# Flamingo block on one core: queries of the cross-attention halved in row layout and turned by DMA instead of on TensorE

## The reference

```python
x = x + tanh(g_xattn) * attention(layernorm(x), ctx, ctx, mask)   # softmax(q k^T / 8 + mask) v, 4 query heads share one k, v
x = x + tanh(g_ffn) * ffn(layernorm(x))                           # router, top 8 of 512 slots, gate
```

## Time and profile before

| | us |
|---|---|
| median of 3 runs (lowest, highest) | 1191.7 (1190.68, 1191.79) |
| the profiled execution | 1189.83 |
| its span | 1187.9 |
| busy in the span: PE, VectorE, ScalarE, GpSimd | 1141.3, 946.4, 918.8, 888.4 |
| first 40 us (loads, first layernorm, pipeline fills): PE busy | 24.39 |
| attention windows 1 to 63, from the first reciprocal L1217 at 39.44 to the last at 885.36 | 845.9 |

### The profile page before, as it was taken

How to read it: one execution, slowest core, us unless ns; L and a number is a source line. 1 busy time by engine, 2 the same in 40 slices (tenths; PEclk the granted TensorE clock), 3 DMA queues, 4 the chain that set the end, 5 groups by cost and what they waited for, 6 DMA issues and landing times.

```text
span 1187.9 us, 35060 instructions
## 1 busy us (share of the span) xinstructions
PE 1141.3 (96%) x14385; PEld 912.3 (77%) x14642; DVE 946.4 (80%) x2255; ACT 918.8 (77%) x1230; POOL 888.4 (75%) x797
## 2 busy tenths in 40 slices
PE   4999999999999999999999999999999999999997
PEld 3888888888888888888888888888877565555553
DVE  5988888887888888888888888888874888766765
ACT  5898998988988898898898889989862344555544
POOL 5999999999999999999999999999970001503222
PEclk9999999999999999999999999999999999999999
DMA  9421231142124213311421221131237100011223
GB/s 340 141 68 48 62 110 54 42 107 71 41 55 103 75 41 68 116 48 41 104 71 52 58 58 42 50 73 47 70 103 262 81 1 1 1 72 72 107 107 142
DMA packets 60735, 95.09 MB, mean 80 GB/s; under 512 B 35233, under 2 KB 44449, under 8 KB 56482
## 3 DMA queue, kind: packets, MB, share of 16 engines
q1 hardware_dynamic: 59858, 91.79, 25.1%
q10 hardware_dynamic: 720, 1.05, 0.3%
HBM read 71.75 MB, written 20.97 MB: 78 GB/s over the span
## 4 chain that ended last, share of the span: by engine, by line
PE 70%; POOL 16%; DVE 8%; issue 3%; ACT 2%; DMA 1%; DVEq 0%; SPq 0%; POOLq 0%
PE psum L913 13%; PE psum L890 12%; POOL arena L577 11%; PE psum L966 8%; PE psum L920 6%; PE psum L901 6%; PE psum L943 6%; PE psum L937 5%; PE psum L938 5%; PE psum L1044 2%; POOL arena L545 2%; PE psum L868 2%; PE psum L953 1%; PE psum L980 1%; POOL arena L594 1%
## 5 line engine op out<-in xcount | busy, mean ns | idle before, releaser
L577 POOL TENSOR_TENSOR arena<-arena 128x768 bf16<-128x768 f32 x448 | 652.6, 1472 | 43.4 <-ACT arena L699 41.5
L1283 DVE CUSTOM_DVE_ANT_0 arena<-psum,arena 128x750 f32<-128x750 f32 x448 | 420.5, 939 | 127.7 <-PE psum L901 122.0
L699 ACT ACTIVATE arena<-psum 128x768 f32<-128x768 f32 x448 | 362.6, 809 | 87.8 <-PE psum L920 87.7
L703 ACT ACTIVATE arena<-arena,neg_max 128x750 f32<-128x750 f32 x448 | 410.9, 917 | 4.2 <-DVE neg_max L1283 4.2
L913 PE MATMUL psum<-ident,arena 128*128 128x128 f32 x1792 | 268.4, 272 | 0.0
L937 PEld LDWEIGHTS psum<-arena 128*128 128x128 bf16 (+1 forms) x2688 | 194.7, 98 | 57.5
L890 PE MATMUL psum<-arena 128*128 128x512 bf16 x674 | 221.9, 383 | 14.2
L938 PE MATMUL psum<-arena 128*128 128x64 bf16 (+1 forms) x2688 | 222.0, 193 | 0.0
L937 PE MATMUL psum<-arena 128*128 128x65 bf16 (+1 forms) x2688 | 221.7, 194 | 0.0
L938 PEld LDWEIGHTS psum<-arena 128*128 128x128 bf16 (+1 forms) x2688 | 178.5, 98 | 53.2
L913 PEld LDWEIGHTS psum<-ident,arena 128*128 128x128 f32 x1792 | 206.3, 140 | 4.3
(11 more groups left out here) (160 smaller groups left out, 1267.6 us busy)
## 6 DMA issues: line engine op xcount, KB each, us to landing
arena<-in_k_t SPq DMA_DIRECT2D x128, 187.5 KB, 3.2
arena<-in_v_rows SPq DMA_DIRECT2D x64, 192.0 KB, 2.5
out<-arena SPq DMA_DIRECT2D x12, 1024.0 KB, 3.9
arena<-in_x_top SPq DMA_DIRECT2D x8, 1024.0 KB, 5.3
arena<-in_x_rest SPq DMA_DIRECT2D x8, 768.0 KB, 4.5
spill<-arena SPq DMA_DIRECT2D x96, 64.0 KB, 2.2
arena<-spill SPq DMA_DIRECT2D x6, 1024.0 KB, 7.2
arena<-in_w_t SPq DMA_DIRECT2D x4, 1024.0 KB, 19.9
```

The costliest lines, as they stand in the source:

```text
L577: pool.tensor_tensor(p_lo[:, n % RING, :], p_sb[:, n % RING, :], high(p_sb[:, n % RING, :]), ALU.subtract).then_inc(p_split, 1)
L699: act.activation(p_sb[:, n % RING, :], flat_ps[:, turned_at(n):turned_at(n) + CW], ACT.Copy).then_inc(evac_a, 1)
L703: act.activation(s_sb[:, n % RING, 0:CTX], s_sb[:, n % RING, 0:CTX], ACT.Exp, bias=neg_max[:, n % 4, :], scale=-1.0).then_inc(exped, 1)
L1283: dve.tensor_tensor_reduce(s_sb[:, n % RING, 0:CTX], flat_ps[:, score_at(n):score_at(n) + CTX], mask_sb[:, max(n % UNITS - REP + 1, 0), :] ...
```

## The change

From the second pair on the queries are no longer turned on PE. In row layout, ScalarE rounds a normalised block of 512 columns straight to bf16 (`round_top`, `round_rest`, m = 5), VectorE computes the same block in f32 into `xn` (`widen`, m = 4) and subtracts the rounded one from it (`halve`, m = 6). High and low half of a head lie side by side in `top_halves` and `rest_halves`, 128 bf16 columns. Transposing DMAs on SP turn them into `q_t`: one of eight 128x128 blocks for a pair's top rows (`turn_top`) and three of two blocks for the rest (`turn_rest`), in odd windows behind the window's loads of k (the rest of every fourth pair one window later). ScalarE's rounding of a top block waits until the former top's DMA has landed. `norm_tasks` says which window works on which block: none in windows 8, 16, ..., one in each other up to 58 except for some at the end, four in window 0 (pair 1 and the whole rest of batch 0); 55 in all, 31 of them tops. GpSimd's three widenings at the start (L570) go. With the freed time VectorE copies the turned probabilities of two units of a group of seven out of PSUM (`evac_on_dve`: units 5 and 0), after the maximum of the same k.

```diff
 def evac_on_dve(n):
-    return False
+    return n % UNITS in (5, 0)
...
-        xn_top = carve("attention", [128, 2, 2 * GW])
-        xn_rest = carve("attention", [128, NB, KV * D])
+        xn = carve("attention", [128, 2 * GW])
+        first_at = used["attention"]
+        first_rest = arena[:, first_at:first_at + NB * 2 * D].rearrange("p (j n) -> p j n", j=NB)
+        top_halves = carve("attention", [128, 2 * REP, 2, D], BF16)
+        rest_halves = carve("attention", [128, NB, KV, 2, D], BF16)
...
-        q_t = carve("attention", [128, 2, 2, UNITS, 128], BF16)
+        q_t = carve("attention", [128, 2, 2 * UNITS, 128], BF16)
...
+        def norm_tasks(window):
+
+            if window == 0:
+                return [(1, 1)] + [(3 + j, 0, j) for j in range(NB)]
+            b, at = divmod(window, KV)
+            later = (window - 3) // KV + 1
+            if window > 0 and at in (1, 2):
+                return [(5, 4 * b + 1 + at)]
+            if window > 0 and later < BATCH:
+                if at == 3:
+                    return [(5, 4 * later)]
+                if at in (4, 5, 6):
+                    return [(5, later, at - 4)]
+                if at == 7:
+                    return [(5, 4 * later + 1)]
+            return []
...
+            def turn_top(pair):
+                sp.wait_ge(top_halved, pair)
+                sp.dma_start_transpose(q_t[:, pair % 2, 0:2 * REP, :], top_halves.rearrange("p h s d -> p (h s d)")).then_inc(top_turned[pair % 2], 16)
+
+            def turn_rest(pair):
+                sp.wait_ge(rest_halved, NB * (pair // 4 + 1))
+                at = 2 * (pair % 4)
+                for j in range(NB):
+                    sp.dma_start_transpose(q_t[:, pair % 2, 2 * REP + 2 * j:2 * REP + 2 * j + 2, :],
+                                           rest_halves[:, j, at:at + 2].rearrange("p h s d -> p (h s d)")).then_inc(rest_turned[pair % 2], 16)
...
+                pair = 1 if window == 0 else (window + 3) // 2
+                if (window == 0 or window % 2 == 1 and window >= 1) and pair < PAIRS:
+                    turn_top(pair)
+                    if pair % 4 != 0:
+                        turn_rest(pair)
+                if window > 0 and window % KV == KV - 2 and window // 2 + 1 < PAIRS:
+                    turn_rest(window // 2 + 1)
...
-            for j in range(NB):
-                pool.tensor_scalar(xn_rest[:, j, 2 * D:], xb[:, 0, j, 2 * D:], ln_scale[:, 1 + j:2 + j], ln_bias[:, 1 + j:2 + j],
-                                   ALU.mult, ALU.add).then_inc(rest_widened, 1)
...
+            def round_top(pair):
                 b, at = pair // 4, pair % 4 * 2 * GW
                 act.wait_ge(ln_done, b + 2 if b else 1)
...
+                if pair >= 2:
+                    act.wait_ge(top_turned[(pair - 1) % 2], 16 * (pair // 2))
+                act.activation(top_halves[:, :, 0, :], xa[:, b, at:at + 2 * GW].rearrange("p (h d) -> p h d", d=D), ACT.Identity,
+                               bias=ln_bias[:, 0:1], scale=ln_scale[:, 0:1]).then_inc(top_rounded, 1)
...
-                if m == 2 and 1 <= window // 2 + 1 < PAIRS:
-                    turn_q(window)
...
+            def widen(block, ahead):
...
+                    dve.tensor_scalar(xn, xa[:, b, at:at + 2 * GW], ln_scale[:, 0:1], ln_bias[:, 0:1], ALU.mult, ALU.add).then_inc(xn_done, 1)
...
+            def halve(index, block):
+
+                dve.wait_ge(xn_done, index + 1)
+                wide = xn.rearrange("p (h d) -> p h d", d=D)
+                if len(block) == 1:
+                    dve.wait_ge(top_rounded, block[0])
+                    dve.tensor_tensor(top_halves[:, :, 1, :], wide, top_halves[:, :, 0, :], ALU.subtract).then_inc(top_halved, 1)
...
-                        dve.tensor_copy(q_t[D * half:D * half + D, pair % 2, half, turns[0]:turns[-1] + 1, :],
-                                        mix_ps[D * half:D * half + D, (window + 1) % 2, 0:128 * len(turns)].rearrange("p (t n) -> p t n", n=128)
-                                        ).then_inc(q_hi_own, 1)
-                if m in (4, 5) and 1 <= pair < PAIRS:
-                    split_q((window + 1) % 2, pair, m - 4, turn_range(window), 2 * (window + 3) + m - 4 + 1)
+                for at, *block in norm_tasks(window):
+                    if m == (at + 1 if window == 0 else at - 1):
+                        widen(block, blocks[-1])
+                    if m == at + 1:
+                        halve(len(blocks) - 1, block)
+                        blocks.append(block)
```

More of the change, by code:

```diff
@@ L873, in score_main @@
                 pair = g // 2
-                half, turn = turned_slot(n)
+                block = query_block(n)
                 if m == 0:
                     pe.wait_ge(k_split, g + 1)
-                if g % 2 == 0 and m in (0, 1):
-                    pe.wait_ge(q_split, queries_before(pair) + m + 1)
+                if (g, m) in ((0, 0), (0, 1)):
+                    pe.wait_ge(q_split, m + 1)
                 if pair == 0 and (g, m) == (0, REP):
@@ L889, in score_main @@
                     kk = high(k_raw[:, g % 2, cols]) if i == 0 else k_lo[:, g % 2, cols]
-                    pe.matmul(flat_ps[:, score_at(n) + cols.start:score_at(n) + cols.stop], q_t[:, pair % 2, half, turn, :], kk,
+                    pe.matmul(flat_ps[:, score_at(n) + cols.start:score_at(n) + cols.stop], q_t[:, pair % 2, block, :], kk,
                               start=(i == 0), stop=(i == 1))
@@ L1189, in _ @@
+            blocks = [[]]
             for c in range(4):
```

154 lines of the change are left out of this document (73 added, 81 removed).

## The result

The changed kernel takes 1208.79 us (median of 4 runs, 1208.27 to 1208.96) against 1191.21 (1190.68 to 1191.79) of the kernel before beside it: ratio 1.0146, 95% interval 1.013 to 1.0162. It is slower by 17.6 us. The forecast was 1195.0, in a range of 1181 to 1220. The sign is as forecast and the size is not: the sum said +3.2, and the span grew from 1187.9 to 1207.1 us, by 19.2.

What follows compares the result with a forecast made beforehand. PE was taken to set the pace, with GpSimd also close to full in windows 4 to 19. Terms 5.6 - 8.8 + 3.0 + 3.4 = +3.2 on 1189.83, plus 1.87 to the median, gave 1195 us, range 1181 to 1220.

Steps and rivals of the forecast that it cites:

- windows 4 to 19: GpSimd needs 215.3 us plus 6.9 for 14 blocks, 222.2 against 216.56: +5.6, upper bound +10.7.
- The price of a block: GpSimd time lost to VectorE per block: 0.17 for the widening plus 0.32 for the halving, 0.49 us; ends 0.17 and 0.86.
- the longest possible: Cap on one VectorE wait for GpSimd: a whole split, 1.4 us.
- Windows 20 to 61: PE's 548.1 us plus factors and wq excess, 555.3 against 564.14: -8.8; VectorE's waits in 34 block windows add +3.4.
- My own sign of being wrong: Prediction wrong if windows 4 to 19 together get shorter, or PE's stops are put down to anything but GpSimd.
- The term for the factors: Windows 27, 35, 43, 51: GpSimd needs 14.52 us, 1.5 too much each, PE regains nothing later: 5.9 us.
- Windows 0 to 3: 1.5 us less for turns, 1.5 more for factors, 3 more (1 to 6) for window 0's four blocks: +3.0.
- The copies: Two VectorE copies of 768 columns a window, 0.88 us each; reach GpSimd some 0.4 us later, covered by the three-deep ring.
- The DMA is late: Rival: an eight-block transpose takes 10 us, not under 6.5; ScalarE and PE stand in seven windows, +24, about 1219; chance 0.12.
- VectorE becomes the bound: Rival: VectorE's two waits come to 1.0 us each, PE waits for maxima in 34 windows, 25 us, 1217; chance 0.09.
- The lock is cheap: Rival: a halving does not hold GpSimd up, a block costs about 0.3 us or less; 1183 to 1188; chance 0.26.
- The full gain: Rival: all 23.7 us of PE's turns are gained, 1168; needs 13.23 us of GpSimd's work in 13.05; given nothing.

Runs made afterwards that it cites:

- e_no_turns: The kernel before without its 217 query turns, their casts and subtractions; every pair multiplies the first pair's queries: 1171.07 us, ratio 0.9837.
- c: The changed kernel with the widening on ScalarE and its f32 result in a free PSUM bank, halving still on VectorE: 1177.42 us, ratio 0.9893.
- j: The changed kernel with both steps still on VectorE, the widening's f32 result put into the free PSUM bank instead of SBUF: 1177.97 us, ratio 0.9893.
- i_w1_not_at_8_16: The changed kernel with w1's splits of windows 8 and 16 moved to windows 22 and 23: 1203.29 us, ratio 1.0103.
- b: The changed kernel with the widening moved to ScalarE, its f32 result still in SBUF, halving still on VectorE: 1204.43 us, ratio 1.0119.
- d: c with all copies of turned probabilities on ScalarE: 1181.81 us, ratio 0.9925.
- f_no_dma: The changed kernel without its transposing DMAs; every pair multiplies the first pair's queries, rounding, widening and halving stay: 1209.48 us, ratio 1.0159.

## Why the prediction was right and where it was wrong

**What bounds the kernel** was read rightly. The two floors of the forecast without any lock are those of the runs: 215.3 us for windows 4 to 19 by GpSimd's work (215.24 in e_no_turns, 215.29 in c and j), 13.05 us for a window by PE's.

**The price of a block** was the main term. I took 0.17 + 0.32 = 0.49 us; measured are 0.19 + 0.45 = 0.64. The widening's was right. For the halving I had one row, L613 held for 0.34, and an argument over the 0.15 us by which it is longer than a widening: it was to end 0.44 us after the release, and it ends 0.55 after. What the runs show is a simple rule: VectorE's instruction ends a fixed time after GpSimd's release (0.28 and 0.55 us), and GpSimd's next one is that much longer less 0.1. In windows 4 to 19 this makes 14 x 0.15 = 2.1 us of the 6.4 by which +12.05 lies above +5.6.

**The rest there** is what no term had: two widenings that are passed over. Windows 9 and 17 last 33.20 us in the change and 27.01 in i_w1_not_at_8_16, 6.2 us (1.0 of it lost clock, half of which window 10 gives back). I had read the row of 3.87 us as one long instruction of GpSimd, as it was, and capped a wait at one split, 1.4 us, "the longest possible". The step that failed is this cap: two more instructions of GpSimd went first here, four in b. The two excesses together are 8.3, since windows 8 and 16 (12.91 us each), window 10 (13.37) and the undisturbed 9 and 17 (13.51 and 13.50 in i) come out 0.3 to 0.5 us shorter each than GpSimd's work in them.

**Windows 20 to 61**: forecast -8.8 + 3.4, measured -0.9. The mechanism of VectorE's waits was right, its size not: I took 0.1 us a window from between 0 and 0.3, and 0.33 is measured in 23 windows (13.38 where the sum has 13.15), +5.2; six windows without a block at 12.79 instead of 13.05 give 1.6 back, and windows 20, 21 and those with the factors add 0.9: together the 4.5 between -5.4 and -0.9. My sum over a window (11.8 + 1.2 = 13.0, "just full") could not tell; the row of maximum, widening, maximum and copy over two units could. My own sign of being wrong, that PE's stops are put down to anything but GpSimd, came true here: from window 20 to 61 PE's weight loads wait 8.0 us for VectorE and 4.7 for GpSimd. VectorE is late there because it waits for GpSimd (in j, with no lock, PE waits for VectorE in none of these windows), so the lock is still the cause, but the path to PE that I had at 0.1 us a window is the main one in these windows. The term for the factors holds (14.76 us against 14.6) but its ground does not: I wrote that PE regains nothing. Without the lock the same work of GpSimd makes those windows 13.09 us (e_no_turns) and 13.45 (c). The three-deep ring carries a surplus over when the neighbours have room, and it was the lock that took the room.

**Windows 0 to 3**: forecast +3.0 (1 to 6 for window 0), measured +8.3. Window 0's four blocks met more waits than 0.3 a step: 1.15 and 1.14 us in two halvings, 1.09 and 0.52 in two widenings, 4 us over the eight steps. With the lock gone, 3.5 of the 7.1 us up to window 1 remain (c). The term is outside its own bounds, and so is that of windows 4 to 19 (12.05 where the upper bound was 10.7). That the whole fell into the range is in part luck: windows 20 to 61 stayed below their upper bound (-0.9 where it was +5.2) and made up for these two.

**The copies** were sized rightly (0.88 us; 462.21 to the next start at 463.08 is 0.87), and taken as covered by the ring where they come late for GpSimd. Of GpSimd's idle time 23.9 us are put down to them, but not as a cost: the changed kernel is faster with them, and so is the one without a lock (c against d).

**The rivals.** *The DMA is late* is refuted twice: by f_no_dma, and by the landing of the eight-block DMAs, which takes 6.7 us once, in window 0, and at most 5.0 in every other window, where 6.5 were allowed. The Trainium skill (VectorE: DVE Perf Modes, The three transpose paths) gives 1309 ns for one block, by which I had estimated 10.5 us for eight in series; the trace doesn't agree, a transposing DMA of eight blocks (256 KB) lands 3.6 us after its issue at the median. The Trainium skill (Advanced Engine Details and Errata, X-Bar Transpose (TRN2)) calls such DMAs as fast as plain ones, and here they nearly are: 256 KB of plain DMA took 3.1. *VectorE becomes the bound* was partly there, as 0.33 instead of 0.75 us a window. *The lock is cheap* is refuted by 0.64. *The full gain* is where it was expected, out of reach: without the lock the kernel ends at 1177 to 1178 (c, j), and the kernel before with the turns simply left out at 1171, not at 1168.

**The lock itself.** In c and j, where each instruction has an operand in PSUM, no split is longer than alone. The Trainium skill (SBUF — State Buffer, Who interferes with whom) says that an instruction of VectorE with at most one SBUF input outside the two-port modes doesn't contend, and that one with two SBUF inputs does; b and c agree. For the widening it names the two-port mode: in SBUF it took 0.54 us and contended, into PSUM 0.81 and did not, which agrees. It also says that issue order decides and that the loser is fully blocked. The runs agree on the blocking, but not on the order: in window 9 two splits that were issued after the widening went before it. By the page's rule I had estimated 1220; the measured 1208.8 lies between that and my 1195: what a held GpSimd instruction loses is what VectorE still has to do after the release, less 0.1, so that a block costs 0.64 and not 1.23.

## What to carry to other kernels

Before work goes to VectorE beside a busy GpSimd, look at where its operands lie: an f32 block handed from one instruction to the next through a free bank of PSUM instead of SBUF made 31 us of 1209 here, with nothing else changed but the waits that guard the bank. Price a wait for a shared port not by one instruction of the other engine but by how many it may have ready, and read VectorE's row of instructions between two results that PE needs, not its sum over a window. When work is spread to where there seems to be room, look at which phase the next window then starts in: five splits put into windows without a block cost more than the spreading freed.

## What the runs showed of the hardware

- An instruction of VectorE that waits for the port ends 0.28 us (widening, 128x512 f32) or 0.55 us (halving) after GpSimd's release, and GpSimd's next one is longer by 0.19 and 0.45. The same 0.19 is paid where the widening itself does not wait (0.54 us long at 163.33 in i).
- VectorE can be passed over by further instructions of GpSimd, none of them delayed: 2.99, 3.88 and 6.69 us were seen for a widening (0.54 alone) and 7.07 for a halving (0.69 alone). In i no instruction was passed over.
- A widening with its result in PSUM takes 0.81 us and in SBUF 0.54, and only the second meets the port.
- A transposing DMA of eight 128x128 bf16 blocks lands in 3.1 us at least, 3.6 at the median, 6.7 at most; one of two blocks in 2.3, 2.4 and 4.5.
- After 2.2 us of standing in 10, PE was granted full clock in one place and 0.84 over the next 10 us in another, in the same kernel; in f_no_dma the two places were exchanged.
